# Windowed attention, one core: scores of a head cut into three products instead of four, and two moves of copies between ScalarE and VectorE

## The chip, the cores and the metric

One core of a Trainium2 chip runs the whole kernel. The metric is device time in microseconds (us), lower is better. Engines in the rows: PE is TensorE's matmul side, PEld its weight loads, ACT ScalarE, DVE VectorE, POOL GpSimd.

## What is computed

The reference passes 16 sequences of 128 tokens of width 128 through a cross-attention block, a six-layer network of windowed attention and feed-forward (called net 0 here), a second cross-attention block and a two-layer network of the same kind (net 1). The change touches net 0. Its attention, cut to what matters (16 heads of 64, window 32):

```python
sim = jnp.einsum('bhwie,bhwje->bhwij', bq, bk2) * QK_SCALE   # a window of queries against its own and the previous window's keys
sim = jnp.where(mask, -jnp.finfo(sim.dtype).max, sim)
attn = jax.nn.softmax(sim, -1)
out = jnp.einsum('bhwij,bhwje->bhwie', attn, bv2)
...
hg = xn @ W1 + b1                                             # the feed-forward layer
a, gate = jnp.split(hg, 2, -1)
return a * jax.nn.gelu(gate, approximate=False) @ W2 + b2
```

So for the 32 queries of a window at most 64 keys count, and the rest of the 128 is masked.

## The kernel before

Everything is fp32 except the mask. Net 0 works on 96 *pairs*: a pair is one sequence in one layer, in two *units* of eight heads (unit 0 and unit 1). Each engine has its own hand-written order of work, a function `step_0(s)`, called for s = 0, 1, 2, ...; in step s the pair s is projected and rotated, pair s-1 normalised, turned (transposed) and scored, pair s-2 gets its softmax, values and output. Engines meet only at semaphores (`wait_ge`, `then_inc`). Inside the steps the feed-forward layer of an earlier group of four sequences is threaded: four steps carry one group, and `ff_phase` gives the position c = 0, 1, 2, 3 in that period (c = 0 mean and variance and the product of the group before, c = 1 the first gate product, c = 2 two more gate products and the three Gelus, c = 3 three up products). Net 0 has 24 such periods.

On PE a step does, for each unit: projections `project_in` (L710, 128x512 each), transposes `turn` (L731, into PSUM banks 5 and 6), `scores_all` (L761 the mask, L767 the products), transposes of the probabilities (L776), `values_all` (L790), and once per step `project_out` (L823). The feed-forward products are L835, L841, L849 (mean, variance, broadcast), L859 (gate), L868 (up), L877 (down).

`scores_all` writes two banks (3 and 4), one for the heads of each half g of the 128 rows. The slot of a query holds 64 keys. A mask product per 32 queries and half puts the mask into the bank; then four products per head: queries 0-31 with keys 0-31, 32-63 with 0-63, 64-95 with 32-95, 96-127 with 64-127. A product of 64 rows by 32 queries stands in the rows as 64\*32, one of 64 by 64 as 64\*64, a full one as 128\*128. Each fp32 product is two matmul records, the bf16 mask product one.

On ACT a step does the exponents (L1578, eight with a sum each), copies of values (L1598), probabilities (L1586), turned q and k (L1555) and outputs (L1609), squares (L1549), and at c = 2 the three Gelus of `ff_gelu` (L1631). Exp and Gelu need different tables, so an ACT_TABLE_LOAD stands before the first Gelu and before the next Exp. On DVE a step does the rotation (L2124, L2129), sums of squares (L2136), row maxima (L2195), a Newton iteration of small instructions (L2162 to L2180) and the feed-forward copies and products (L2252, L2258, L2264). POOL does L1924, L1931 and L1938 on SBUF data.

Waits that matter below: the value projection of unit 0 on PE waits for `AT["oe"][0]`, that is ACT's `outputs` of unit 0; `scores_all(1, s-2)` waits for `AG["ex"][0]`, that is ACT's exponents of unit 0; `values_all(0, s-2)` waits for the turned k of unit 1 being copied out of bank 6; ACT's `outputs` wait for `values_all`.

Of the kernel before, what the change touches and what calls it, by code (L numbers as in the profile page):

```python
# [14 lines left out]
P = 128  # L15
# [48 lines left out]
def build(nc, A, out):  # L64
# [9 lines left out]
    with ExitStack() as ctx:  # L74
# [501 lines left out]
        def _(pe):  # L576
# [125 lines left out]
            def pe_phase(ph):  # L702
# [48 lines left out]
                def scores_all(i, p):  # L751

                    if p == 0:
                        pe.wait_ge(YP["we"], 2)
                    pe.wait_ge(AT["qte"][i], p + 1)
                    pe.wait_ge(AT["kte"][i], p + 1)
                    for q in range(0, P, 32):
                        for g in range(2):
                            rows = slice(DH * g, DH * g + DH)
                            own = ident_b[rows, DH * g + q % DH:DH * g + q % DH + 32]  # L760
                            nc.tensor.matmul(bank[3 + g][q:q + 32, 0:256], own, mask_b[0][rows, q // DH], start=True, stop=False)  # L761
                    pieces = [(0, 0, 32), (32, 0, 64), (64, 32, 64), (96, 64, 64)]
                    for j in range(4):
                        for q, key, n in pieces:
                            for g in range(2):
                                rows = slice(DH * g, DH * g + DH)
                                mm = nc.tensor.matmul(bank[3 + g][q:q + 32, DH * j:DH * j + n],  # L767
                                                      q_t[i][rows, P * j + q:P * j + q + 32], k_t[i][rows, P * j + key:P * j + key + n],
                                                      start=False, stop=j == 3)
                    mm.then_inc(AT["s"], 1)  # L770

# [679 lines left out]
        def _(act):  # L1451
# [89 lines left out]
            def act_phase(ph):  # L1541
# [58 lines left out]
                def outputs(i, p):  # L1600

                    act.wait_ge(AT["o"][i], p + 1)
                    if ni == 0:
                        at(act, AT["y"][0], p)
                    else:
                        at(act, AT["y"][i], nth(i, p - 1))
                    if ni == 0:
                        for half in range(2):
                            ins = nc.scalar.activation(o_t[i][:, 256 * half:256 * half + 256], bank[7 - half][:, 0:256], ACT.Copy)  # L1609
                        ins.then_inc(AT["oe"][i], 1)  # L1610
                    else:
                        nc.scalar.activation(o_t[i], bank[7][:], ACT.Copy).then_inc(AT["oe"][i], 1)
# [11 lines left out]
                    nc.scalar.activation(fxn, fxn, ACT.Identity, scale=lnp[w][:, 0:1], bias=lnp[w][:, 1:2]  # L1624
                                         ).then_inc(FF["aff"], 1)

                def ff_gelu(f):
                    for c in range(3):
                        w = CH[c][1]
                        act.wait_ge(FF["ge"], 3 * f + c + 1)  # L1630
                        nc.scalar.activation(gl[c][0:w, :], gl[c][0:w, :], ACT.Gelu, bias=b1[f // 4 % 2][0:w, 3 + c:4 + c]  # L1631
                                             ).then_inc(FF["gelu"], 1)

                def step_0(s):
                    c, f, before = ff_phase(ph, s)
                    if live(s - 2):
                        exponents_all(0, s - 2)
                        values(0, s - 2)
                    if live(s - 3):
                        probs_all(1, s - 3)  # L1640
                    if live(s):
                        square(0, s, 1)
                        square(0, s, 0)
                    if s == 0:
                        gate_weights()
                    if live(s - 1):
                        turned(0, s - 1, 0)
                    if live(s - 3):
                        outputs(1, s - 3)
                    if s in (1, 3, 5):  # L1650
                        g_square(act, (s + 1) // 2, (s + 1) // 2)
                    if c == 0 and f >= 0:
                        ff_square(f)
                    if c == 1 and f >= 0:
                        ff_affine(f)
                    if live(s - 2):
                        exponents_all(1, s - 2)
                    if live(s):
                        square(1, s, 1)
                        square(1, s, 0)  # L1660
                    if live(s - 1):
                        turned(0, s - 1, 1)
                    if s == hi:
                        for k in range(2):
                            g_square(act, 4 + k, k)
                    if live(s - 2):
                        probs_all(0, s - 2)
                        values(1, s - 2)
                    if live(s - 1):
                        turned(1, s - 1, 1)  # L1670
                        turned(1, s - 1, 0)
                    if c == 2 and f >= 0:
                        ff_gelu(f)
                    if live(s - 2):
                        outputs(0, s - 2)

                def step_1(s):
                    c, f, before = ff_phase(ph, s)
                    if live(s - 3):
                        outputs(1, s - 3)  # L1680
                    if live(s - 2):
                        exponents(1, s - 2, 0)
                        probs(0, s - 2, 0)
                        exponents(1, s - 2, 1)
                    if live(s):
                        square(0, s, 0)
                    if live(s - 1):
                        turned(0, s - 1, 0)
                        turned(0, s - 1, 1)
                    if s - lo in (1, 3):  # L1690
                        n = 10 + (s - lo - 1) // 2
                        g_square(act, n, n - 8)
                    if c == 0 and f >= 0:
                        ff_square(f)
                    if live(s):
                        square(0, s, 1)
                    if live(s - 2):
                        values(0, s - 2)
                        probs(0, s - 2, 1)
                    if c == 1 and f >= 0:  # L1700
                        ff_gelu(f)
                    if live(s - 1):
                        exponents(0, s - 1, 1)
                        exponents(0, s - 1, 0)
                    if live(s - 2):
                        probs(1, s - 2, 1)
                        probs(1, s - 2, 0)
                    if live(s):
                        square(1, s, 0)
                    if c == 0 and f >= 0:  # L1710
                        ff_affine(f)
                    if live(s - 2):
                        values(1, s - 2)
                    if live(s - 1):
                        turned(1, s - 1, 1)
                    if live(s):
                        square(1, s, 1)
                    if live(s - 1):
                        turned(1, s - 1, 0)
                    if live(s - 2):  # L1720
                        outputs(0, s - 2)
# [104 lines left out]
            def between(s, part):  # L1826

                if (s, part) == (1, 1):
                    ff0_square(23)
                if (s, part) == (2, 1):  # L1830
                    ff0_affine(23)
                    g_square(act, 6, 2)
                if (s, part) == (3, 2):
                    ff0_gelu(23)
                if (s, part) == (5, 1):
                    g_square(act, 7, 3)
                if s in (7, 9) and part == 0:
                    n = 8 + (s - 7) // 2
                    g_square(act, n, n - 8)
# [194 lines left out]
        def _(dve):  # L2034
# [76 lines left out]
            def dve_phase(ph):  # L2111
# [22 lines left out]
                def sum_squares(i, p, c):  # L2134
                    dve.wait_ge(AT["sqk" if c else "sqq"], un(i, p))
                    nc.vector.tensor_reduce(ss[:, i, HU * c:HU * c + HU], heads(sq[i][c]), AX.X, ALU.add  # L2136
                                            ).then_inc(AT["ssk" if c else "ssq"], 1)

                def ff_done(s):

                    c, f, before = ff_phase(ph, s)
                    if f < 0 or c < 0:
                        at(dve, FF["z"], before + 1)
                    elif ni == 0 and c == 0:
                        dve.wait_ge(FF["rstd"], RSQ * (f + 1))
                    elif c == (3 if ni == 0 else 1):
                        dve.wait_ge(FF["hid"], 3 * f + 3)
                    else:
                        dve.wait_ge(FF["ge"], 3 * f + (3 if c == 2 else 1))
# [177 lines left out]
                def step_0(s):  # L2327
# [32 lines left out]
                    if live(s):  # L2360
                        sum_squares(1, s, 0)
                        sum_squares(1, s, 1)
                    feed_forward_0(s, 2)
                    if live(s):
                        newton(s, 0, 3)
                    if live(s - 1):
# [331 lines left out]
```

## Time and profile before

| what | us |
|---|---|
| median of three runs | 2304.53 (2298.14 to 2307.23) |
| the profiled execution | 2299.02 |
| its span | 2297.2 |
| PE busy in the span | 2124.9 |
| DVE, ACT, POOL busy | 1760.9, 1712.2, 1340.2 |

The profile page gives busy time, share and instructions of each engine over the whole span; the other views are cut to a stretch or an engine. In a timeline a row is a run of like instructions: start, length from the first start to the last end, engine, line, operation, tiles, shape, count, and in brackets the idle time before it with what ended it ("issue" means that no wait of the profile explains it). Ends of matmuls are modelled, so starts are the safer figures.

### The profile page before, as it was taken

The page shows a single profiled execution, that of the slowest core. Times are in us where ns is not written, and L with a number is a line of the kernel's source. Part 1 is how long each engine was busy: PE and PEld are TensorE (multiplying, and loading weights), DVE is VectorE, ACT ScalarE, POOL GpSimd, SP SyncE. Part 2 cuts the span into 40 slices and gives each one's busy share as a digit, 9 for nine tenths or more (in the row PEclk, how much of TensorE's full clock was granted, in tenths as well). Part 3 has the DMA queues.
Part 4 walks back from the last instruction along what each step waited for, and adds up shares of the span by engine and source line. Part 5 has one row for each costly group of instructions (what it writes and reads, how often), then busy time and mean ns, then how long its engine had stood idle before and what let it go on. Part 6 is the DMA issues. An engine that isn't in the chain of part 4 may idle for free. (4 is left out here: it accounts for less than half of the span.)

```text
span 2297.2 us, 88445 instructions
## 1 busy us (share of the span) xinstructions
PE 2124.9 (93%) x33790; PEld 1456.7 (63%) x33790; DVE 1760.9 (77%) x4953; ACT 1712.2 (75%) x5916; POOL 1340.2 (58%) x1270
## 2 busy tenths in 40 slices
PE   7988999999999999999999999999999886899997
PEld 5656666666666666666666666666666564666665
DVE  4988877778777878777778777877777478788873
ACT  3767788787787877787887777887788543778784
POOL 1337666666666666665676566666666124766660
PEclk8999999999999999999999999999999998999999
DMA  4001221112211222112211122111221100000001
GB/s 112 4 3 39 70 58 45 41 46 67 57 43 39 64 51 57 39 43 61 57 46 42 43 65 60 46 39 45 52 53 43 48 10 10 13 13 16 13 9 28
DMA packets 144799, 96.93 MB, mean 42 GB/s; under 512 B 61976, under 2 KB 137408, under 8 KB 144384
## 3 DMA queue, kind: packets, MB, share of 16 engines
q1 hardware_dynamic: 143232, 91.02, 15.5%
q8 instruction: 274, 4.49, 0.8%
q14 instruction: 141, 1.16, 0.2%
q10 hardware_dynamic: 1152, 0.26, 0.1%
HBM read 23.11 MB, written 1.05 MB: 11 GB/s over the span
## 5 line engine op out<-in xcount | busy, mean ns | idle before, releaser
L710 PE MATMUL bank<-wqkv,hs 128*128 128x512 f32 x1344 | 666.7, 614 | 19.3 <-ACT arena L1609 13.7
L1931 POOL TENSOR_TENSOR arena<-arena,rnorm 128x512 f32<-128x512 f32 x448 | 455.5, 1046 | 388.5 <-DVE rnorm L2180 387.3
L1924 POOL TENSOR_TENSOR arena<-arena 128x512 f32<-128x512 f32 x448 | 568.0, 1275 | 132.5 <-DVE arena L2129 132.2
L1578 ACT ACTIVATE arena<-bank,amx 128x64 f32<-128x64 f32 x1536 | 458.8, 336 | 8.5 <-DVE amx L2195 8.3
L2124 DVE TENSOR_TENSOR arena<-bank,rot 128x512 f32<-128x512 f32 x448 | 306.9, 685 | 82.7 <-PE bank L710 79.0
L1555 ACT ACTIVATE arena<-bank 128x512 f32<-128x512 f32 x448 | 264.4, 617 | 132.0 <-PE bank L731 130.9
L710 PEld LDWEIGHTS bank<-wqkv,hs 128*128 128x128 f32 x1344 | 228.6, 191 | 203.8 <-issue 154.9
L1578 ACT ACTIVATION_READ_ACCUMULATOR arena<-bank,amx 128x1 f32 x1536 | 352.3, 229 | 0.0
L2129 DVE TENSOR_TENSOR arena<-bank,rot 128x256 f32<-128x256 f32 x896 | 334.0, 414 | 0.0
L731 PEld LDWEIGHTS bank<-ident,arena 128*128 128x128 f32 x1792 | 212.6, 142 | 152.8 <-issue 128.3
L2136 DVE TENSOR_REDUCE ss<-arena 128x8 f32<-128x512 f32 x448 | 283.4, 670 | 32.5 <-ACT arena L1549 32.3
L1549 ACT ACTIVATE arena<-bank 128x512 f32<-128x512 f32 x448 | 265.9, 647 | 42.0 <-DVE arena L2129 41.2
L1938 POOL TENSOR_TENSOR arena<-arena,ainv 128x512 f32<-128x512 f32 x192 | 200.7, 1045 | 164.9 <-DVE ainv L2203 164.7
L731 PE MATMUL bank<-ident,arena 128*128 128x128 f32 x1792 | 251.5, 274 | 14.1 <-POOL arena L1931 6.4
L1609 ACT ACTIVATE arena<-bank 128x256 f32<-128x256 f32 x384 | 127.2, 387 | 174.6 <-PE bank L790 173.7
L823 PEld LDWEIGHTS bank<-arena,wo 128*128 128x128 f32 x1792 | 221.6, 194 | 55.1 <-issue 48.1
L790 PE MATMUL bank<-arena 64*64 64x32 f32 (+1 forms) x9216 | 186.1, 221 | 49.0 <-issue 47.6
L823 PE MATMUL bank<-arena,wo 128*128 128x128 f32 x1792 | 226.9, 279 | 3.0 <-ACT arena L1609 2.6
L790 PEld LDWEIGHTS bank<-arena 64*64 64x64 f32 x9216 | 160.6, 134 | 71.0 <-issue 54.5
L2195 DVE TENSOR_REDUCE amx<-bank 128x4 f32<-128x256 f32 x384 | 143.8, 416 | 39.8 <-PE bank L767 39.2
L767 PE MATMUL bank<-arena 64*32 64x64 f32 (+1 forms) x12288 | 168.8, 217 | 0.0
L767 PEld LDWEIGHTS bank<-arena 64*32 64x32 f32 x12288 | 154.9, 105 | 0.3
(213 smaller groups left out, 3229.8 us busy)
## 6 DMA issues: line engine op xcount, KB each, us to landing
arena<-arena SPq DMA_DIRECT2D x768, 64.0 KB
wqkv<-in_L_ffn_Wqkv_dram SPq DMA_DIRECT2D x24, 256.0 KB
hs<-z SPq DMA_DIRECT2D x128, 32.0 KB, 1.8
hs<-z SPq DMA_DIRECT2D x128, 31.8 KB, 1.9
fx<-z SPq DMA_DIRECT2D x31, 128.0 KB, 2.2
fx<-z SPq DMA_DIRECT2D x31, 127.0 KB, 2.5
wqkv<-in_L_ffn_Wqkv_dram SPq DMA_DIRECT2D x24, 128.0 KB
w<-in_L_ffn_W_dram SPq DMA_DIRECT2D x6, 341.0 KB
```

The costliest lines, as they stand in the source:

```text
L710: nc.tensor.matmul(bank[o][:], src[:], wqkv[w][:, off:off + 512], start=True, stop=True).then_inc(AT[name] if part < 2 else AT[name][i], 1)
L731: mm = nc.tensor.transpose(bank4[o][:, j, :], rc[i][c][p % 2][:, j * P:(j + 1) * P], ident[:])
L767: mm = nc.tensor.matmul(bank[3 + g][q:q + 32, DH * j:DH * j + n], q_t[i][rows, P * j + q:P * j + q + 32], k_t[i][rows, P * j + key:P * j + ...
L790: mm = nc.tensor.matmul(bank4[7 - half][to:to + DH, j, q0:q1], src[g][rows, DH * h:DH * h + DH], pbt[i][0][rows, h * P + q0:h * P + q1], s ...
L823: mm = nc.tensor.matmul(bank4[7][:, 0, :], wo[w][:, i, j, :] if ni == 0 else wo[w][:, j // 2, j % 2, :], o_t[i][:, j * P:(j + 1) * P], sta ...
L1549: nc.scalar.activation(sq[i][c], bank[c][:], ACT.Square).then_inc(AT["sqk" if c else "sqq"], 1)
L1578: ins = nc.scalar.activation(pb[i][0][p % 2][:, h * DH:(h + 1) * DH], bank[3 + g][:, j * DH:(j + 1) * DH], ACT.Exp, bias=amx[p % 2][:, i, ...
L1924: nc.gpsimd.tensor_tensor(t, t, rs[i][c], ALU.add).then_inc(AT["ak" if c else "aq"][i], 1)
L1931: nc.gpsimd.tensor_tensor(t, t, rnorm[p % 2][:, i, HU * c:HU * c + HU].unsqueeze(2).to_broadcast([P, HU, DH]), ALU.mult).then_inc(AT["mk" ...
L2124: nc.vector.tensor_tensor(heads(rc[i][c][p % 2]), src, r[:, 2 * c, :].unsqueeze(1).to_broadcast([P, HU, DH]), ALU.mult)
L2129: ins = nc.vector.tensor_tensor(dst, src[:, :, (1 - a) * hd:(2 - a) * hd], r[:, 2 * c + 1, a * hd:(a + 1) * hd].unsqueeze(1).to_broadcast( ...
L2136: nc.vector.tensor_reduce(ss[:, i, HU * c:HU * c + HU], heads(sq[i][c]), AX.X, ALU.add).then_inc(AT["ssk" if c else "ssq"], 1)
```

## The change

Three edits. First, `scores_all`: two mask products of 64 queries in place of four of 32 for each half, and three products per head in place of four; queries 0-63 are now one product with keys 0-63, the other two pieces of 32 queries stay. Second, ACT at c = 2: the output copies of unit 0 stand between the first and the second Gelu, not behind the third. Third, at c = 2 the two copies of turned q and k of unit 1 leave ACT and are done by VectorE, ahead of its Newton iteration (22 steps). The other changed lines only call `ff_gelu` chunk by chunk.

```diff
@@ PE, scores_all
-                    for q in range(0, P, 32):
+                    for q in range(0, P, DH):
                         for g in range(2):
                             rows = slice(DH * g, DH * g + DH)
-                            own = ident_b[rows, DH * g + q % DH:DH * g + q % DH + 32]
-                            nc.tensor.matmul(bank[3 + g][q:q + 32, 0:256], own, mask_b[0][rows, q // DH], start=True, stop=False)
-                    pieces = [(0, 0, 32), (32, 0, 64), (64, 32, 64), (96, 64, 64)]
+                            nc.tensor.matmul(bank[3 + g][q:q + DH, 0:256], ident_b[rows, rows], mask_b[0][rows, q // DH], start=True, stop=False)
+                    pieces = [(0, DH, 0), (64, 32, 32), (96, 32, 64)]
                     for j in range(4):
-                        for q, key, n in pieces:
+                        for q, m, key in pieces:
                             for g in range(2):
                                 rows = slice(DH * g, DH * g + DH)
-                                mm = nc.tensor.matmul(bank[3 + g][q:q + 32, DH * j:DH * j + n],
-                                                      q_t[i][rows, P * j + q:P * j + q + 32], k_t[i][rows, P * j + key:P * j + key + n],
+                                mm = nc.tensor.matmul(bank[3 + g][q:q + m, DH * j:DH * j + DH],
+                                                      q_t[i][rows, P * j + q:P * j + q + m], k_t[i][rows, P * j + key:P * j + key + DH],
                                                       start=False, stop=j == 3)
@@ ACT, step_0
-                    if live(s - 1):
+                    if live(s - 1) and not (c == 2 and f >= 0):
                         turned(1, s - 1, 1)
                         turned(1, s - 1, 0)
                     if c == 2 and f >= 0:
-                        ff_gelu(f)
+                        ff_gelu(f, 0)
                     if live(s - 2):
                         outputs(0, s - 2)
+                    if c == 2 and f >= 0:
+                        ff_gelu(f, 1)
+                        ff_gelu(f, 2)
@@ DVE
+                def turned(p, c):
+
+                    dve.wait_ge(AT["kt" if c else "qt"][1], p + 1)
+                    at(dve, AT["s"], un(1, p - 1))
+                    nc.vector.tensor_copy((k_t if c else q_t)[1], bank[5 + c][:]).then_inc(AT["kte" if c else "qte"][1], 1)
...
                     feed_forward_0(s, 2)
+                    if s >= 7 and (s - 7) % 4 == 2 and live(s - 1):
+                        turned(s - 1, 1)
+                        turned(s - 1, 0)
                     if live(s):
                         newton(s, 0, 3)
```

## Rows read from the trace of the kernel before

**Rows 1.** The page's busy times of the whole span.

```profile
PE 2124.9 (93%) x33790; PEld 1456.7 (63%) x33790; DVE 1760.9 (77%) x4953; ACT 1712.2 (75%) x5916; POOL 1340.2 (58%) x1270
```

**Rows 2.** Timeline of PE: project_out of one step each (start us, length).

```profile
200.11 1.95 PE L823 MATMUL bank<-arena,wo 128*128 128x128 f32 x16
...
739.44 1.95 PE L823 MATMUL bank<-arena,wo 128*128 128x128 f32 x16
...
757.28 1.95 PE L823 MATMUL bank<-arena,wo 128*128 128x128 f32 x16
...
772.53 1.95 PE L823 MATMUL bank<-arena,wo 128*128 128x128 f32 x16
...
790.15 1.95 PE L823 MATMUL bank<-arena,wo 128*128 128x128 f32 x16
...
806.20 1.95 PE L823 MATMUL bank<-arena,wo 128*128 128x128 f32 x16
...
1822.37 2.02 PE L823 MATMUL bank<-arena,wo 128*128 128x128 f32 x16 [0.86 <-ACT arena L1609]
```

**Rows 3.** Timeline of PE, c = 2 into c = 3.

```profile
778.85 0.53 PE L790 MATMUL bank<-arena 64*64 64x64 f32 x18
780.49 0.66 PE L790 MATMUL bank<-arena 64*64 64x32 f32 x30 [1.11 <-issue]
...
786.37 0.30 PE L761 MATMUL bank<-mask_b,ident_b 64*32 64x256 bf16 x8 [0.70 <-issue]
```

**Rows 4.** Timeline of ACT, the same stretch and the next outputs.

```profile
777.60 1.08 ACT L1555 ACTIVATE arena<-bank 128x512 f32<-128x512 f32 x2
...
779.99 1.95 ACT L1631 ACTIVATE arena<-arena,b 128x512 f32<-128x512 f32 x3
781.84 0.63 ACT L1609 ACTIVATE arena<-bank 128x256 f32<-128x256 f32 x2
782.49 1.28 ACT L1578 ACT_TABLE_LOAD   x1
...
786.12 0.64 ACT L1598 ACTIVATE arena<-bank 128x512 f32<-128x512 f32 x1
...
798.22 0.66 ACT L1609 ACTIVATE arena<-bank 128x256 f32<-128x256 f32 x2 [1.10 <-PE bank L790]
```

**Rows 5.** Who PE waited for (us in all, times, longest).

```profile
PE bank L790 <- issue: 47.6, 65, 3.1
```

**Rows 6.** DMA queues of the page: packets, MB, share of 16 engines.

```profile
q8 instruction: 274, 4.49, 0.8%
```

**Rows 7.** Timeline of PE at c = 3: where the product's shape changes and where not.

```profile
795.39 1.04 PE L731 MATMUL bank<-ident,arena 128*128 128x128 f32 x8
796.36 0.30 PE L761 MATMUL bank<-mask_b,ident_b 64*32 64x256 bf16 x8
...
797.25 0.90 PE L790 MATMUL bank<-arena 64*64 64x64 f32 x48
...
800.76 0.60 PE L776 MATMUL bank<-ident,arena 128*128 128x128 f32 x4
801.19 1.02 PE L835 MATMUL bank<-fx,mean_w 128*128 128x512 f32 x2
```

**Rows 8.** Timeline of PE in net 1, full shape into 64 by 64.

```profile
2050.14 0.60 PE L798 MATMUL bank<-ident,arena 128*128 128x128 f32 x4
2050.67 0.41 PE L741 MATMUL bank<-mask_b,ident_b 64*64 64x512 bf16 x4
```

**Rows 9.** Weight loads of the score products: count, busy us, mean ns, idle before.

```profile
L767 PEld LDWEIGHTS bank<-arena 64*32 64x32 f32 x12288 | 154.9, 105 | 0.3
```

**Rows 10.** Busy time by stretch: length, PE, PEld, DVE, ACT, POOL, PE clock, DMA.

```profile
1060.00:1063.90 3.90, 1.91 (x101) 1.63 (x87) 2.42 (x5) 1.97 (x5) 2.33 (x3) 0.86 0.22 55
1063.90:1067.50 3.60, 3.60 (x7) 1.51 (x5) 1.35 (x3) 3.10 (x19) 0.03 (x1) 0.50 0.16 41
```

**Rows 11.** Groups of DVE: the copy nearest to the moved ones.

```profile
L2252 DVE COPY arena<-bank 128x512 f32<-128x512 f32 (+1 forms) x91 | 61.8, 679 | 33.2 <-PE bank L859 33.2
```

More of the change, by code:

```diff
@@ L1625, in ff_affine, with ff_gelu @@
                                          ).then_inc(FF["aff"], 1)
[L1627 to L1632, printed above, removed]
+                def ff_gelu(f, c):
+                    w = CH[c][1]
+                    act.wait_ge(FF["ge"], 3 * f + c + 1)
+                    nc.scalar.activation(gl[c][0:w, :], gl[c][0:w, :], ACT.Gelu, bias=b1[f // 4 % 2][0:w, 3 + c:4 + c]
+                                         ).then_inc(FF["gelu"], 1)
                 def step_0(s):
@@ L1700, in step_1 @@
                     if c == 1 and f >= 0:
-                        ff_gelu(f)
+                        for chunk in range(3):
+                            ff_gelu(f, chunk)
                     if live(s - 1):
@@ L1833, in between @@
                 if (s, part) == (3, 2):
-                    ff0_gelu(23)
+                    for c in range(3):
+                        ff0_gelu(23, c)
                 if (s, part) == (5, 1):
```

## Prediction

> **What bounds the kernel now.** I read the page first. PE is busy 93% of the span, the next engine 77% [rows 1]; the feed-forward steps on ACT and DVE matter only where PE is seen to wait. Next I laid PE's timeline out by step, with `project_out` as the mark [rows 2]. One period of four steps without disturbance runs from 739.44 to 806.20: 17.84 us (c = 0 into 1), 15.25 (1 into 2), 17.62 (2 into 3), 16.05 (3 into 0), together 66.76. The second and the third interval hold two 512-column feed-forward products each, yet differ by 2.37 us. The reader is to see why in the next two views. PE stands 0.70 us before the scores of unit 1 [rows 3], and ACT works without a pause from the turned copies at 777.60 over Gelu, outputs and a table load to the last exponent at about 786.12 [rows 4]; the scores start 0.25 later. So this one interval is set by ACT, the other three by PE.
>
> A second loss shows in the waits: PE stopped 65 times, 47.6 us in all, at L790 with no wait to explain it [rows 5], as at 780.49, in the middle of 48 matmuls that have no semaphore between them [rows 3]. The instruction queue moved 274 packets of 16.4 KB [rows 6] for 67,580 PE records [rows 1], some 247 records a packet. Scores and values together are 240 records, loads counted, within about 1.8 us (0.89 and 0.90 [rows 7]), the densest place of the program, and the stops come at their end. I read them as PE waiting for instructions. How much it costs: 95 intervals from 200.11 to 1822.37 average 17.08, that is 68.31 a period against 66.76 clean; times 23.75 periods, 37 us (stops within the ACT-bound interval cost nothing).
>
> **The change, part by part: scores.** There are 192 calls, eight in a period. A call has 72 matmul records now (8 mask, 64 products); it will have 52 (4 and 48). The loaded weight columns of the products stay the same: 64 times 32 now, 16 times 64 and 32 times 32 after. From mask to values a call takes 0.89 us now [rows 7]. But the three pieces no longer have one shape: 64\*64 for queries 0-63, 64\*32 for the other two, in turn, four times. That makes seven changes of shape inside a call where there is none now.
>
> What does a change of shape cost? Four transposes followed by a product of the same shape take 0.43 (800.76 to 801.19); eight followed by the 64\*32 mask take 0.97 where twice 0.43 is 0.87 [rows 7]; four followed by a 64\*64 mask take 0.53 [rows 8]. So about 0.10 into either narrow shape; no row isolates a change between the two narrow ones. The Trainium skill says the same of the rule behind it (TensorEngine Tiling (Array Packing), Key Properties: changing the tiling mode, "not just tile", drains TensorE); the trace agrees with its 0.10 at block borders, and no row shows it inside a block. By the page, this edit loses; by its second point, that tiles operate independently, it would not, which is the first rival below.
>
> Cost of a call after. A stretch between two changes is two passes over 64 columns on each of its tiles: L835 makes 0.43 per 512-column record (801.19, two records to the next mark of like length), so 0.054 per pass, 0.11 together; plus 0.09 to 0.10 for the change; plus the opening weight load, which nothing covers any more. That load is nowhere seen alone: at least nothing, at most its whole 105 ns [rows 9]; I take 0.05, half, since the first pass can begin on the first tile while the others load. A stretch is then 0.25 (0.20 to 0.30). Masks 0.12 (estimate: their 256 one-pass columns are a quarter of an fp32 record's 0.43), first passes 0.11, seven stretches 1.75, closing change 0.10: 2.08 against 0.89, so 1.2 more per call (0.84 to 1.54). The floor below that, if only the seven changes count and the rest overlaps as today, is 7 times 0.09, 0.63.
>
> **Outputs and turned copies.** ACT gives up 1.08 us of copies [rows 4]; Gelu 0 would end near 779.5. The outputs, though, need the values of unit 0, which start at 778.85 now [rows 3] and at 780.05 with scores 1.2 longer; outputs start 0.97 after values (797.25 to 798.22) [rows 4, 7], at 781.02. So ACT, in order, idles 1.5 with Gelu 1 and 2 queued behind the outputs; then outputs 0.65, two Gelus 1.23 (two thirds of 1.85), table load and exponents 3.63 [rows 4]: done at 786.53 against 786.12. What the copies save is eaten by the place of the outputs. No table load is added: Copy stands behind Gelu today without one of its own [rows 4].
>
> VectorE gets two copies of 0.68 [rows 11], ahead of `newton` and `row_max_all(0)`. Its row maxima wait for the scores, which come 1.2 later, so the 1.36 lies under that wait; if that cover were gone, 22 steps of 1.36 would be 30 us at most. POOL's normalisation starts later by the same and is needed by PE only after the next step's projections, six records of 0.43. `values_all(0)` needs the k copy, and this is done before the scores end.
>
> **The sum.** Three PE-bound intervals get two longer calls each: 17.84, 15.25 and 16.05 become 20.24, 17.65 and 18.45. The ACT-bound one gets 0.41 before the scores and 1.2 for them: 17.62 becomes 19.23. Together 75.57 against 66.76, 8.81 a period, 211 us in 24. The instruction stops should go: 200 records in 3.0 us, half the rate; minus 37. The profiled execution's 2299 becomes 2473. Its median stands 5 above it; I say 2475. With 0.84 a call, the same working gives 18.51 for the ACT-bound interval, 72.69, plus 142 less 37: 2404. With 0.63: 71.01, 2364. With 1.54: 78.29, 2539.
>
> The Trainium skill calls the crossing of a 16 KiB instruction block mostly hidden (Runtime: NRT & Kernel Launch, Instruction fetch mechanics). The 47.6 us speak against that here; by the page, the 37 would have another cause and stay, 2510.
>
> **Rivals.** First, on the other side: a 64\*64 tile on columns 0-63 and 64\*32 tiles on columns 64-127 never overlap, and if PE drains only where tiles overlap, the seven changes are free. Then fewer records save between nothing (same loaded columns) and 0.25 (20 of 72 records of 0.89); say 0.11. PE-bound intervals fall 0.22 each, the ACT-bound one by 0.9 (copies gone, outputs wait little) and 0.11, 1.67 a period, 40 us; half the instruction stops go, 18 more: 2241. For it: the disjoint columns. Against it: every change of shape in rows 7 and 8 costs the same 0.10, whichever way. It decides below about 0.3 a call, three paid changes: there the period's loss equals copies and stops. Second, the clock: after a stretch with PE busy 1.91 of 3.90 us the granted clock was 0.50 (1.2 GHz, against 2.4) for the next 3.60 [rows 10], whose work takes 1.80 at the full clock. If the thin scores bring that once a period, 24 times 1.80, 43 more: 2518. Against it: PE stays active between the changes. Third, half-paid changes near the point of balance: no change that can be measured.
>
> **How the numbers follow.** Changes paid in full without the clock 0.72, with the clock 0.10, free 0.14, balanced 0.04. So slower 0.82, same 0.04, faster 0.14, with 0.5% (11.5 us) as the least that a measurement of this kernel can tell from no change. The paid cases run from 2364 to 2539, with the clock at the long end to 2582; I take 2340 (the floor, and no instruction stop hidden today) to 2560, which leaves out the free case and the tails. That is the likeliest case's own range too.
>
> **What would show it.** Right: L767 in two shapes, mask to values near 2 us, loads of L767 with idle time before them, stops at L790 mostly gone, ACT idle before L1609 at c = 2, the DVE copies of q and k over before the scores end. Wrong: mask to values at or below 0.9; or a period under 66.76.

## The result, and the profile after

The change makes the kernel slower: 2460.47 us (2456.44 to 2473.36, median of 4 runs) against 2305.88 beside it, a ratio of 1.0691 with a 95% interval of [1.0651, 1.0732]. The forecast was 2475 us, 2340 to 2560. The profiled execution took 2461.42 us with a span of 2459.6.

The page of the kernel after, its busy times and its instruction queue (beside [rows 1, 6]), and two groups of its instructions:

```profile
PE 2348.5 (95%) x29950; PEld 1586.3 (64%) x29950; DVE 1800.1 (73%) x4997; ACT 1689.1 (69%) x5872; POOL 1341.9 (55%) x1270
...
q8 instruction: 244, 4.00, 0.7%
...
L766 PEld LDWEIGHTS bank<-arena 64*32 64x32 f32 (+1 forms) x9216 | 278.9, 114 | 105.0 <-issue 0.5
...
L1608 ACT ACTIVATE arena<-bank 128x256 f32<-128x256 f32 x384 | 126.3, 381 | 355.4 <-PE bank L789 355.4
```

PE has 3,840 matmul records fewer (as many loads fewer) and 224 us more of busy time. The instruction queue moved 30 packets fewer for these 7,680 records, 256 a packet, so it is PE's. With fewer records and more busy time, the records that are left have become dearer. The loads of the score products, now L766, stand behind 105.0 us of idle time. ACT waits 355 us ahead of the output copies where it waited 175.

What PE waited for in the kernel after (us in total, times, longest; beside [rows 5]):

```profile
PE bank L760 <- issue: 28.9, 22, 1.3
```

The stops at the values (47.6 us of before) have no row any more. L760, the mask of unit 1 at c = 2, waits for the exponents: 1.3 us, once a period.

PE's timeline from `project_out` at c = 0 to the next one, kernel after (start, us, engine, line, operation; beside [rows 2, 7]; the view ends within the last row):

```profile
793.69 1.95 PE L822 MATMUL bank<-arena,wo 128*128 128x128 f32 x16
...
801.60 0.30 PE L760 MATMUL bank<-mask_b,ident_b 64*64 64x256 bf16 x4
801.74 2.05 PE L766 MATMUL bank<-arena 64*64 64x64 f32 x48
803.71 0.90 PE L789 MATMUL bank<-arena 64*64 64x64 f32 x48
...
808.62 0.30 PE L760 MATMUL bank<-mask_b,ident_b 64*64 64x256 bf16 x4
810.73 0.90 PE L789 MATMUL bank<-arena 64*64 64x64 f32 x48
...
813.39 0.38 PE L822 MATMUL bank<-arena,wo 128*128 128x128 f32 x2
```

From mask to values it is 2.11 us in both calls (801.60 to 803.71, 808.62 to 810.73), as in 185 of the 192 calls. Before, the fastest calls took 0.89 (66 of the 192) and the others mostly 0.92 to 1.13. The four intervals of a period are 19.70, 17.55, 18.93 and 18.41, together 74.59 against 66.76 clean, and nearly all periods from the second on repeat them. From the first to the last `project_out` that makes 1776.4 us against 1622.3, 154.1 more. The sum: 7.83 a period times 23.75 is 186; before's excess over its clean period, 37, is gone; after has an excess of 5 of its own, 19 from falls of the clock (below) less 14 for shorter steps at both ends. The rest of the 162 between the two profiled executions, 8, lies ahead of and behind these steps.

ACT at c = 2 of the kernel after, and PE at the end of ACT's run (beside [rows 3, 4]):

```profile
837.43 0.72 ACT L1630 ACTIVATE arena<-arena,b 128x512 f32<-128x512 f32 x1
839.36 0.66 ACT L1608 ACTIVATE arena<-bank 128x256 f32<-128x256 f32 x2 [1.21 <-PE bank L789]
839.90 1.32 ACT L1630 ACTIVATE arena<-arena,b 128x512 f32<-128x512 f32 x2
841.24 1.28 ACT L1577 ACT_TABLE_LOAD   x1
...
845.11 0.30 PE L760 MATMUL bank<-mask_b,ident_b 64*64 64x256 bf16 x4 [1.31 <-issue]
```

Between the first and the second Gelu, ACT stands 1.21 us for the values of unit 0, and PE stands 1.31 us later for the exponents that ACT makes after them.

### The profile page after: what moved, and what is told of

Same layout as the page of the kernel before. It is cut to its first block and busy times, and to the rows that moved or that the text cites. A ratio compares the mean times of both kernels' runs of the same rounds, so it can differ in the third digit from the quotient of the medians.

```text
span 2459.6 us, 80765 instructions
## 1 busy us (share of the span) xinstructions
PE 2348.5 (95%) x29950; PEld 1586.3 (64%) x29950; DVE 1800.1 (73%) x4997; ACT 1689.1 (69%) x5872; POOL 1341.9 (55%) x1270
## 5 line engine op out<-in xcount | busy, mean ns | idle before, releaser
L710 PE MATMUL bank<-wqkv,hs 128*128 128x512 f32 x1344 | 673.8, 622 | 5.2 <-ACT arena L1548 2.8
L766 PE MATMUL bank<-arena 64*32 64x64 f32 (+1 forms) x9216 | 395.3, 232 | 0.0
L710 PEld LDWEIGHTS bank<-wqkv,hs 128*128 128x128 f32 x1344 | 234.0, 194 | 184.0 <-issue 162.7
L766 PEld LDWEIGHTS bank<-arena 64*32 64x32 f32 (+1 forms) x9216 | 278.9, 114 | 105.0 <-issue 0.5
L1554 ACT ACTIVATE arena<-bank 128x512 f32<-128x512 f32 x404 | 242.6, 624 | 135.8 <-PE bank L731 134.7
L1548 ACT ACTIVATE arena<-bank 128x512 f32<-128x512 f32 x448 | 265.1, 649 | 41.5 <-DVE arena L2133 41.1
L789 PE MATMUL bank<-arena 64*64 64x32 f32 (+1 forms) x9216 | 176.9, 223 | 1.9 <-ACT arena L1585 1.2
L789 PEld LDWEIGHTS bank<-arena 64*64 64x64 f32 x9216 | 155.5, 137 | 21.2 <-issue 2.8
```

The source lines that it names most:

```text
L710: nc.tensor.matmul(bank[o][:], src[:], wqkv[w][:, off:off + 512], start=True, stop=True).then_inc(AT[name] if part < 2 else AT[name][i], 1)
L766: mm = nc.tensor.matmul(bank[3 + g][q:q + m, DH * j:DH * j + DH], q_t[i][rows, P * j + q:P * j + q + m], k_t[i][rows, P * j + key:P * j + ...
L789: mm = nc.tensor.matmul(bank4[7 - half][to:to + DH, j, q0:q1], src[g][rows, DH * h:DH * h + DH], pbt[i][0][rows, h * P + q0:h * P + q1], s ...
L1548: nc.scalar.activation(sq[i][c], bank[c][:], ACT.Square).then_inc(AT["sqk" if c else "sqq"], 1)
```

## The experiments

All kernels below do the whole computation. Theory A throughout is that of the forecast: a change of product shape has a price, and the place of the outputs makes ACT wait. Their times, ratios to the kernel before with 95% intervals, and readings:

| kernel | changes among the products | mask to values, us | time, us | ratio |
|---|---|---|---|---|
| whole change | 7 | 2.11 | 2460.5 | 1.0691 [1.0651, 1.0732] |
| 1 scores alone | 7 | 2.11 | 2443.5 | 1.0599 [1.0571, 1.0626] |
| 2 moves alone | 0 | 0.89 at best | 2302.4 | 0.9991 [0.997, 1.0011] |
| 3 grouped | 1 | 1.27 | 2294.9 | 0.9961 [0.9942, 0.9979] |
| 4 one shape | 0 (1 from the masks) | 1.02 | 2296.3 | 0.9949 [0.9932, 0.9966] |
| 5 three | 3 | 1.55 | 2338.0 | 1.0155 [1.0133, 1.0178] |
| 6 fifteen | 15 | 3.98 | 3184.1 | 1.3832 [1.379, 1.3874] |
| 7 grouped, no moves | 1 | 1.27 | 2299.5 | 0.9995 [0.9984, 1.0007] |
| 8 grouped, outputs last | 1 | 1.27 | 2282.3 | 0.9917 [0.9898, 0.9936] |
| 9 narrow first | 1 | 1.15 | 2283.1 | 0.9919 [0.9902, 0.9936] |
| 10 narrow first, outputs last | 1 | 1.15 | 2270.4 | 0.9879 [0.986, 0.9898] |
| 11 whole change, outputs last | 7 | 2.11 | 2411.5 | 1.0489 [1.0472, 1.0506] |

Mask to values is what most calls of a kernel take. Outside the times expected came kernels 1 (6 us under), 2 (10 over), 5 (2 under), 6 (far over), 7 (3 under), 9 (3 over) and 11 (8 under); kernel 8 came out 4 us under its one figure.

**1 and 2: the two halves of the change.** Kernel 1 is the kernel before with the new `scores_all` alone, kernel 2 the kernel after with the old one.

> The kernel before with only the new scores_all; outputs stay behind the third Gelu and ACT makes all turned copies. Theory A, changes of product shape are paid: mask to values 2.1 us as with the whole change, three intervals of a period as there (19.7, 17.6, 18.4), the one from c = 2 to c = 3 at 17.62 + 1.2 = 18.8; 2450 to 2470 us. Rival B, the loss is made by the moves on ACT and VectorE: 2280 to 2320 us, mask to values near 0.9.

> The kernel before with only the moves (outputs between first and second Gelu, VectorE's copies); scores as before. Theory A: only the interval from c = 2 to c = 3 changes; ACT saves 1.08 of copies and idles some 0.3 before the outputs, so 17.62 becomes about 16.85, 18 us in 24 periods; stops of PE without a wait inside that interval, so far hidden under ACT, now count: 2280 to 2292 us. Rival B: above 2400 us, ACT idle before the outputs 1 us a period or more.

The loss is in the scores: alone they cost 6.0%, and rival B falls. Kernel 1 has intervals of 19.70, 17.55, 18.59 and 18.41 (forecast for the third: 18.8). Its scores of unit 1 at c = 2, where PE has waited 0.97 us, and the values after them:

```profile
770.41 0.30 PE L760 MATMUL bank<-mask_b,ident_b 64*64 64x256 bf16 x4 [0.97 <-issue]
...
772.52 0.90 PE L789 MATMUL bank<-arena 64*64 64x64 f32 x48
```

The moves cost a further 17 us on top of the new scores (21 by the two ratios).

With the old scores they gain nothing that can be measured, though the interval from c = 2 to c = 3 fell as expected where it ran clean, to 16.83. Its mean over the phase is 17.70 against 17.77 before. Where the gain went stands in PE's waits and timeline of kernel 2, and in its windows (span in us, PE and PEld busy, DVE, ACT, POOL, granted clock, DMA share, GB/s) of that interval, three times:

```profile
PE bank L790 <- issue: 47.4, 64, 2.2
...
780.87 0.66 PE L790 MATMUL bank<-arena 64*64 64x32 f32 x30 [1.11 <-issue]
...
787.34 0.30 PE L761 MATMUL bank<-mask_b,ident_b 64*32 64x256 bf16 x8 [1.30 <-issue]
...
706.43:723.25 16.82, 15.34 (x298) 10.59 (x296) 13.86 (x39) 15.37 (x50) 11.20 (x11) 1.00 0.12 28
772.90:791.12 18.22, 15.64 (x297) 10.78 (x296) 13.95 (x39) 15.37 (x50) 12.38 (x12) 1.00 0.21 60
841.96:861.84 19.88, 16.80 (x298) 11.11 (x297) 14.76 (x41) 17.03 (x62) 12.28 (x13) 0.94 0.18 49
```

The stops at the values are all still there. In the interval shown by the timeline rows (772.90 to 791.12) one of 1.11 us stands in the values of unit 0, and with the outputs ahead of two Gelus it delays everything that ACT does after them: 18.22 instead of 16.82, where the kernel before, with the same stop, had its 17.62. So five of 22 such intervals take 17.9 to 18.5 at a full clock, and five more 19.9 to 22.3 with a mean clock of 0.89 to 0.94. The kernel before has 17 such intervals at 17.62 and five at 19.2 to 21.7, only one of them with a lower clock.

**3, 5 and 6: how many changes of shape.** The same 52 records in another order. Kernel 3:

```diff
-                    for j in range(4):
-                        for q, m, key in pieces:
-                            for g in range(2):
+                    for j, (q, m, key) in [(j, x) for part in (pieces[:1], pieces[1:]) for j in range(4) for x in part]:
+                        for g in range(2):
```

> The whole change, but all four 64*64 products of each row group first and then all 64*32 products: the same 52 records and the same arithmetic, one change of shape among the products in place of seven. Theory A, price per change: mask to values 1.0 to 1.25 us; a period some 68.2; stops half gone; 2290 to 2330 us. Rival C, the price is that of products which no longer run side by side on all tiles, or of the 64*64 product itself, whatever their order: mask to values 2.0 to 2.1 us and 2450 to 2470 us. Rival D, changes between disjoint tiles cost nothing: no difference from the whole change, 2461 us.

Kernel 5 does this for two heads and then for the other two:

```diff
+                    for j, (q, m, key) in [(j, x) for two in ((0, 1), (2, 3)) for part in (pieces[:1], pieces[1:]) for j in two for x in part]:
```

> The whole change, with the heads taken in two pairs: 64*64 products of heads 0 and 1, then their 64*32 products, then the same for 2 and 3. Three changes of shape among the products, in place of seven or one. Theory A, a price per change: by the 1.27 us of one change and the 2.11 of seven, 0.14 each, mask to values 1.55 us; by the 166 us between those two kernels, 28 us for each change in a call, 2350 us (2340 to 2362). Rival E, the price comes with the first few changes or only when every head alternates: 1.3 us and 2300, or 2.0 and 2440.

Kernel 6 puts the loop over the row groups g outside that over the pieces:

```diff
                     for j in range(4):
-                        for q, m, key in pieces:
-                            for g in range(2):
+                        for g in range(2):
+                            for q, m, key in pieces:
```

> The whole change, but the two row groups one after the other within each head: 64*64, two 64*32, then the other group's 64*64, two 64*32. Fifteen changes in a call. Theory A1, each change costs 0.14 by itself: mask to values 2.11 + 8 * 0.14 = 3.2 us, 2680 us. Theory A2, the forecast's stretch: what costs is a stretch between two changes, 0.25 us with its passes and its opening load, even if only one row group works in it: 16 * 0.25 + 0.2 = 4.2 us, 2860 us. Rival C, no price per change: 2.1 us and 2461 us.

A call of kernel 3, then the loads of its products and PE's stops at the values:

```profile
778.17 0.30 PE L760 MATMUL bank<-mask_b,ident_b 64*64 64x256 bf16 x4
778.30 1.21 PE L765 MATMUL bank<-arena 64*64 64x64 f32 x48
779.44 0.90 PE L788 MATMUL bank<-arena 64*64 64x64 f32 x48
...
L765 PEld LDWEIGHTS bank<-arena 64*64 64x64 f32 (+1 forms) x9216 | 209.3, 116 | 13.0
...
PE bank L788 <- issue: 5.2, 8, 1.2
```

The same of kernel 5:

```profile
776.62 0.30 PE L760 MATMUL bank<-mask_b,ident_b 64*64 64x256 bf16 x4
776.75 1.49 PE L765 MATMUL bank<-arena 64*64 64x64 f32 x48
778.17 0.90 PE L788 MATMUL bank<-arena 64*64 64x64 f32 x48
...
L765 PEld LDWEIGHTS bank<-arena 64*32 64x32 f32 (+1 forms) x9216 | 232.1, 115 | 43.6 <-issue 0.2
```

The same products on the same tiles take 1.27, 1.55 and 2.11 us with one, three and seven changes: 0.14 us a change, on a straight line. Rivals D and E fall, and C falls as the price of the whole; the tiles of the two shapes share no column, and the price of a change is there all the same. But carried back to no change at all the line gives 1.13 us, 0.24 above the fastest calls of before, so a fifth of the 1.22 does not go with the number of changes. Kernel 4 below, with all pieces in one shape, lacks this part (1.02 with one change). What is left of rival C would make it: products of two shapes that no longer run side by side, as the forecast's sum had them, pass after pass. No run takes that part by itself. The idle time ahead of the loads says where it arises: 13.0 us over 192 changes, 43.6 over 576 and 105.0 over 1,344, 0.07 to 0.08 each. Before PE loads a weight of another shape it waits about that long; the other half of the 0.14 fits the opening load that nothing covers, which the runs don't separate. The times, 2294.9, 2338.0 and 2460.5, follow with 22 and 31 us a change; kernel 5 came out 2 us under the range expected.

The Trainium skill (TensorEngine Tiling (Array Packing), Key Properties) has the rule that changing the mode, and not just the tile, drains TensorE. The runs agree: 0.14 us for it here, and nothing for alternating among tiles of one shape (kernel 4).

Kernel 6 went by A2 in its call and beyond both in its time. Its windows (us, then PE and PEld busy, DVE, ACT, POOL, granted clock, DMA share, GB/s):

```profile
775.37:779.35 3.98, 3.98 (x54) 2.71 (x53) 1.54 (x3) 0.92 (x2) 3.23 (x3) 1.00 0.32 83
779.35:780.80 1.45, 1.45 (x53) 1.39 (x49) 0.76 (x2) 0.00 (x0) 0.00 (x0) 0.50 0.49 139
```

A call takes 3.98 us at the full clock, 1.87 more for eight stretches, 0.23 each; A2 had 4.2, A1 3.2. The two row groups no longer run side by side, so their passes add to the changes. After the call the granted clock is 0.50, 1.2 GHz, and the values take 1.45 us instead of 0.83; this comes back at call after call. The period is 105.81 against 74.59, 31.2 more, of which 8 times 1.87 is 15.0. The other 16.2 fit the work at the lower clock: the mean granted clock of a steady period is 0.82, and over the 192 calls it falls 187 times. So the clock rival of the forecast is a real mechanism. It was not set off by the 2.11 us calls of the whole change where nothing else made PE idle.

**4: the same arithmetic in one shape.**

```diff
-                    pieces = [(0, DH, 0), (64, 32, 32), (96, 32, 64)]
+                    pieces = [(0, 32, 0), (32, 32, 0), (64, 32, 32), (96, 32, 64)]
```

> The whole change, but each 64*64 product split into two 64*32 products (queries 0-31 and 32-63, the same 64 keys), taken in the same order: the same arithmetic, 68 records, no change of shape among the products, one between masks and products. Theory A: mask to values 0.95 to 1.05 us, 2280 to 2300 us. Rival B, the moves: above 2400 us. If the cost lay in products of 64 keys for queries 0-31: mask to values above 1.3 us.

A call of kernel 4 and its stops:

```profile
791.39 0.30 PE L760 MATMUL bank<-mask_b,ident_b 64*64 64x256 bf16 x4
791.63 0.86 PE L766 MATMUL bank<-arena 64*32 64x64 f32 x64
792.42 0.90 PE L789 MATMUL bank<-arena 64*64 64x64 f32 x48
...
PE bank L789 <- issue: 30.6, 34, 1.7
```

The 64 products begin 0.24 after the masks, where kernel 3 has 0.13 (the one change of shape), and take 0.79 to the values, as before (0.77 to 0.86), although their order alternates among the same pieces. Sixteen records more than the whole change, and 164 us less: the changes of shape count here and not the number of records.

**7, 8 and 11: what each of the moves does.** In kernels 8 and 11 `outputs(0, s - 2)` stands behind the third Gelu again; kernel 7 has neither move.

```diff
                     if c == 2 and f >= 0:
                         ff_gelu(f, 0)
+                        ff_gelu(f, 1)
+                        ff_gelu(f, 2)
                     if live(s - 2):
                         outputs(0, s - 2)
-                    if c == 2 and f >= 0:
-                        ff_gelu(f, 1)
-                        ff_gelu(f, 2)
```

> The kernel before with only the grouped scores (one change among the products); ACT makes all turned copies and the outputs stand behind the third Gelu. Beside the kernel with grouped products and VectorE's copies (outputs last), it tells what the copies are worth. ACT has 1.08 us more before its exponents at c = 2, so the interval from c = 2 to c = 3 goes from 16.79 to between 17.6 and 17.9, 20 to 26 us in 24 periods: 2302 to 2308 us if the copies gain; 2280 to 2286 us if they are worth nothing.

> The products grouped by shape (one change), VectorE's copies kept, but the output copies of unit 0 behind the third Gelu again. ACT's wait before these outputs at c = 2, 0.37 us there, goes; the interval from c = 2 to c = 3 falls from 17.27 to 16.9, 9 us in 24 periods: 2286 us, if the place of the outputs costs and only VectorE's copies gain. If the early outputs are what gains: 2295 to 2312 us.

> The whole change with its seven changes of shape, only the outputs of unit 0 behind the third Gelu again. The forecast's step: the early place makes ACT wait (1.21 us at c = 2 in the trace of the whole change) and that eats what the copies save. If so, PE's 1.31 us before the scores falls to 0.1 or 0.2 and the interval from c = 2 to c = 3 from 18.93 to about 17.8, 27 us in 24 periods, and the falls of the clock that stand only in this interval go with the wait, some 12 us: 2420 to 2436 us. Rival: the early place costs nothing, 2455 to 2465 us.

ACT in kernel 8 at c = 2, where the outputs follow the third Gelu without a wait:

```profile
772.41 1.95 ACT L1629 ACTIVATE arena<-arena,b 128x512 f32<-128x512 f32 x3
774.26 0.63 ACT L1607 ACTIVATE arena<-bank 128x256 f32<-128x256 f32 x2
```

The interval from c = 2 to c = 3 is 17.76 in kernel 7, 16.79 in kernel 8 with VectorE's copies and 17.27 in kernel 3 with both moves. So the copies on VectorE gain 0.97 a period (17 us by the times), and the early place of the outputs gives 0.48 of it, 12.5 us, back. With the whole change the same place costs far more: kernel 11 is 49 us faster than it (46 by the ratios). The interval falls from 18.93 to 17.73, as expected; times 24 that is 29. The other 20, expected as 12, are mostly the falls of the clock: the whole change has seven before its last two steps, each in this interval, and kernel 11 has none. Kernel 1, whose PE waits 0.97 us there, has seven too, shorter ones of 1.6 us each. Beside it, kernel 11 shows the copies alone with the new scores: 32 us gained (25 by the ratios), these falls included. One fall in windows of the whole change:

```profile
918.00:921.40 3.40, 2.09 (x46) 1.40 (x46) 1.28 (x4) 3.40 (x17) 3.40 (x4) 1.00 0.03 8
921.40:925.00 3.60, 3.60 (x62) 2.57 (x63) 1.64 (x4) 2.01 (x10) 1.84 (x2) 0.50 0.32 82
925.00:928.00 3.00, 3.00 (x8) 1.61 (x7) 2.05 (x5) 2.25 (x13) 0.96 (x1) 0.50 0.03 7
```

PE stands 1.31 us for ACT, then does thin scores, and the granted clock is 0.50 from then on; this interval and the next together are 3.2 us longer than the clean ones (five times; 1.6 the other two, 19 us in all).

**9 and 10: the order that is left.** The narrow pieces come first, each shape behind its own masks, so that the 64\*64 products end next to the values, which are 64\*64 too.

```diff
+                    wide, narrow = [(0, DH, 0)], [(64, 32, 32), (96, 32, 64)]
+                    for part in (narrow, wide):
+                        for q, m, key in part:
+                            for g in range(2):
...
+                                own = ident_b[rows, DH * g + q % DH:DH * g + q % DH + m]
+                                nc.tensor.matmul(bank[3 + g][q:q + m, 0:256], own, mask_b[0][rows, q // DH], start=True, stop=False)
+                        for j, (q, m, key) in [(j, x) for j in range(4) for x in part]:
```

> The whole change, grouped, but the 64*32 pieces first (their masks as 64*32 as well) and the 64*64 mask and products last, next to the values, which are 64*64 too. One change in all between scores and values, in place of two (one among the products, one from 64*32 to the values); 54 records instead of 52. Theory A: 0.14 less a call, mask to values 1.13 us, intervals of 17.8, 15.6, 17.0 and 16.5, 27 us in 24 periods: 2268 us (2262 to 2280), or some more if stops in front of the values come back. Rival: the change into the values is free, mask to values 1.27 or more, 2295 us.

> 64*32 pieces first, 64*64 pieces next to the values, VectorE's copies, outputs of unit 0 behind the third Gelu: the two steps that each gained against the grouped order, together. The place of the outputs was worth 12.5 us and the order 11.8; at c = 2 to c = 3 ACT's wait before the outputs is already shorter with this order, so not the whole sum: that interval 16.7 in place of 17.14, 10 us: 2270 to 2275 us. If both remove the same wait: 2281 us.

A call of kernel 10:

```profile
752.27 0.29 PE L763 MATMUL bank<-mask_b,ident_b 64*32 64x256 bf16 x4
752.39 0.62 PE L767 MATMUL bank<-arena 64*32 64x64 f32 x32
752.94 0.30 PE L763 MATMUL bank<-mask_b,ident_b 64*64 64x256 bf16 x2
753.07 0.57 PE L767 MATMUL bank<-arena 64*64 64x64 f32 x14
753.42 0.27 PE L790 MATMUL bank<-arena 64*64 64x64 f32 x2
753.48 0.22 PE L767 MATMUL bank<-arena 64*64 64x64 f32 x2
753.53 0.84 PE L790 MATMUL bank<-arena 64*64 64x64 f32 x46
```

The first values start 1.15 us after the masks, among the last products. But all values except the first two records start only 1.26 after the masks, and the intervals fell by 0.07 a call (15.88 to 15.73, 16.74 to 16.59), not by 0.14: half a change, 12 us and not 27. Which part is given back, the masks in two shapes or the overlap of products and values, no run tells. Kernel 10 took 2270.4 us, within its range: 1.2% under the kernel before and 7.7% under the whole change, with the fewer records and VectorE's copies of the change, one change of shape and the outputs where they were.

## Why the prediction was right, step by step

- **Scores.** The forecast gave a call 2.08 us; it takes 2.11. The working holds too: a stretch at 0.25 is about what kernel 6 shows (0.23 for one more, 16 in 3.98), and 0.14 of it is the change with its opening load, which the forecast had at 0.09 to 0.10 plus 0.05. That 0.05 was half of what lay between two bounds, so that the sum came this close is luck in part. The 0.10 was read from changes out of the full shape into a narrow one; its rows have no change back into the full shape and none between two narrow ones, so the "whichever way" among the rivals was not read from them. And 0.89 is the fastest call: the clean period before has two of them, five of 0.96 to 0.98 and one of 1.13, so a call really adds 1.14 on average.
- **Intervals bound by PE.** Forecast 20.24, 17.65 and 18.45; measured 19.70, 17.55 and 18.41. The first is the term that was mis-sized. Its 17.84 was taken as PE's own, but 0.29 of it was PE waiting for POOL ahead of the transposes (the first row below, of the kernel before), and the steps around it were drawn out by 0.20. Its two calls took 0.89 and 0.98 (753.64 to 754.62), so two of 2.11 add 2.35; the longer first call covers the 0.49, and the interval grew by 1.86 and not by 2.4.

```profile
753.08 0.63 PE L731 MATMUL bank<-ident,arena 128*128 128x128 f32 x4 [0.29 <-POOL arena L1931]
753.64 0.30 PE L761 MATMUL bank<-mask_b,ident_b 64*32 64x256 bf16 x8
...
754.62 0.90 PE L790 MATMUL bank<-arena 64*64 64x64 f32 x48
...
787.50 0.90 PE L790 MATMUL bank<-arena 64*64 64x64 f32 x48 [0.18 <-issue]
```

- **The interval bound by ACT.** Forecast 19.23, measured 18.93. The scores of unit 1 start 0.33 later than before, counted from the interval's start (14.17 against 13.84; forecast 0.41). The scores themselves add 0.98 and not 1.2, since this call took 1.13 before, with a pause of 0.18 ahead of the values (last row above). That the outputs' place eats what the copies save is shown by kernels 1, 3, 7, 8 and 11: half of it with the grouped scores, and more than it with the whole change, 49 us against 32.
- **Stops at the values.** All gone, as forecast, and with them the rival by which the 37 us stay (2510). The 37 are the excess of the whole phase before and hold three falls of the clock and shorter steps at its ends beside the stops. The number of stops follows the density of the records and not their count: 64 with 240 records in some 1.8 us (kernel 2), 34 with 232 in 1.9 (kernel 4), 9 and 11 with 204 in 2.05 (kernels 9 and 10), 8 with 200 in 2.2 (kernel 3), three with the same 200 in 2.45 (kernel 5), none in 3.0. That PE waits there for its instructions also stands in the packets of the instruction queue, which the prediction didn't look at one by one: all 44 stops of the kernel before that are longer than 0.2 us (43.9 of the 47.6 us) end 1.2 to 1.6 us after a packet has ended (the one up to 780.49 after a packet that ended at 779.15), as do the 32 such stops of kernel 4 and the 8 of kernel 3. A moment taken at random stands so in 7 of 100 cases. The 21 shorter stops of before, 3.7 us in all, mostly don't go with the packets. The rule of the Trainium skill (Runtime: NRT & Kernel Launch, Instruction fetch mechanics) that a block crossing is mostly hidden holds here for the looser records (some 230 of the 274 packets come without such a stop) and not for the densest ones.
- **VectorE's copies** lie under the wait for the scores, as forecast. In VectorE's timeline of the kernel after they are over at 837.24, and the row maxima stand 0.73 us later on for the scores. The copies are the one part of the change that gains by itself.

```profile
835.95 1.29 DVE L2147 COPY arena<-bank 128x512 f32<-128x512 f32 x2 [0.23 <-PE bank L731]
...
838.53 0.76 DVE L2205 TENSOR_REDUCE amx<-bank 128x4 f32<-128x256 f32 x2 [0.73 <-PE bank L766]
```

- **Rivals.** Free changes of shape fell with kernels 3 to 5. The clock falls seven times in the ACT-bound interval and not once a period, 19 us where the rival had 43.

Against the profiled execution the forecast was 12 us too high: 25 too much from the intervals (0.98 a period in 24, and 24 periods for 23.75), less 5 for the excess that the kernel after has of its own and 8 ahead of and behind the steps. So errors that the working didn't foresee cancel in part; that the time came out within 1% is luck to that extent.

## What to carry to other kernels

Count the changes of tile shape that a loop's order makes, not only its instructions: the same products cost 1.27 or 2.11 us by their order alone, and fewer, larger products in two shapes lost to more of one. Where an in-order engine gets a step that waits for another engine's longest step, price what is queued behind it: here the place of two small copies was worth 12 us with short scores and 49 with long ones. A kernel that is slow for one reason can hide a good part: take the change apart before dropping it.

## What was not expected of the hardware

- Thin work without any wait in PE's rows brings TensorE's clock down: in kernel 6 PE is busy 3.98 of 3.98 us at the full clock by the profile, and yet the granted clock is 0.50 after it (mean of the run 0.852, against 0.978 for the whole change). A PE that counts as busy in the profile, where ends are modelled, is not enough to keep it up.
- A change of shape costs 0.14 us, opening load included, between shapes on columns that don't overlap. That is no less than the 0.10 to 0.11 at borders between blocks of work whose columns do overlap ([rows 7, 8], kernel 4).
